# Graph attention, second sweep: edge product with edges on partitions, gathered rows added by VectorE

## What is computed

```python
h = layernorm(x) * gamma + beta
x_j, x_i = h[src], h[dst]
t = gelu(concat([x_j, edge_vector], 1) @ Wt + bt)
q = x_i @ Wq + bq
k = t @ Wk + bk
attn = sum(k * q, -1) * edge_type / sqrt(D)
m = segment_max(attn, dst)
e = exp(attn - m[dst])
a = e / (segment_sum(e, dst) + 1e-16)
aggr = segment_sum(a * (t @ Wv + bv), dst)
return residual + gelu(aggr)
```

## Time and profile before

| what | value |
|---|---|
| median of 3 runs | 4536.91 us (4527.91 to 4538.68) |
| profiled execution | 4530.53 us |
| its span, first to last instruction | 4528.9 us |
| TensorE busy, weight loads | 76%, 59% |
| GpSimd, VectorE, ScalarE busy | 68%, 42%, 35% |
| mean granted TensorE clock | 0.748 |
| DMA | 99 GB/s on average |

### The profile page before, as it was taken

How to read it: one execution, slowest core, us unless ns; L and a number is a source line. 1 busy time by engine, 2 the same in 40 slices (tenths; PEclk the granted TensorE clock), 3 DMA queues, 4 the chain that set the end, 5 groups by cost and what they waited for, 6 DMA issues and landing times. The chain is left out here.

```text
span 4528.9 us, 75426 instructions
## 1 busy us (share of the span) xinstructions
PE 3448.6 (76%) x19146; PEld 2674.6 (59%) x19147; DVE 1900.2 (42%) x6965; ACT 1604.3 (35%) x3258; POOL 3095.4 (68%) x3340
## 2 busy tenths in 40 slices
PE   1477677777767677675878888888888888888887
PEld 1356555555555555553666666666666666666665
DVE  5333222222222222223555555555555554545544
ACT  5433222222222222223434334334334334343343
POOL 7467777777777777774766666666666666666662
PEclk5566555555555655656999999999999999899998
DMA  5223323333233232333444434444434434444442
GB/s 159 66 75 85 80 76 80 78 77 80 75 80 79 77 80 75 80 79 85 124 112 115 118 115 115 117 115 116 117 113 117 118 110 120 109 116 117 114 115 67
DMA packets 390323, 446.83 MB, mean 99 GB/s; under 512 B 111896, under 2 KB 314862, under 8 KB 390256
## 3 DMA queue, kind: packets, MB, share of 16 engines
q0 software_dynamic: 100352, 205.72, 18.3%
q1 hardware_dynamic: 276940, 233.83, 17.4%
q10 hardware_dynamic: 12964, 6.53, 0.5%
HBM read 387.58 MB, written 58.21 MB: 98 GB/s over the span
## 5 line engine op out<-in xcount | busy, mean ns | idle before, releaser
L513 POOL DMA_INDIRECT attention_t<-source_rows,attention_idx x1552 | 1536.1, 990 | 493.9 <-issue 492.8
L513 POOL DMA_INDIRECT gin_hs<-h_rows,gin_idx x1472 | 1407.0, 956 | 435.8 <-issue 435.8
L678 PE MATMUL gin_sums<-gin_hot,gin_hs 128*128 128x40 f32 x3136 | 684.8, 412 | 0.0
L678 PEld LDWEIGHTS gin_sums<-gin_hot,gin_hs 128*128 128x128 f32 x3136 | 670.3, 329 | 22.4 <-issue 21.7
L1206 ACT ACTIVATE attention_tT<-attention_pre_ps 128x512 f32<-128x512 f32 x392 | 234.0, 597 | 1229.1 <-PE attention_pre_ps L1096 1229.0
L1096 PE MATMUL attention_pre_ps<-attention_evT,attention_w_edge 128*128 128x512 f32 x784 | 466.6, 681 | 2.6 <-DMA attention_evT<-in_edge_attr_cols 2.6
L1119 PE MATMUL attention_sc_q<-attention_qw,attention_tT 128*128 x3136 | 419.0, 278 | 0.0
L1119 PEld LDWEIGHTS attention_sc_q<-attention_qw,attention_tT 128*128 128x128 f32 x3136 | 400.1, 200 | 0.0
L1153 PE MATMUL attention_sum_ps<-attention_e_hot,attention_t 128*128 128x96 f32 x3136 | 389.1, 284 | 0.0
L1153 PEld LDWEIGHTS attention_sum_ps<-attention_e_hot,attention_t 128*128 128x128 f32 x3136 | 373.1, 199 | 12.3 <-issue 0.2
L1351 DVE TENSOR_TENSOR attention_masked<-attention_masked,attention_row_bank 128x80 f32<-128x80 f32 x784 | 126.3, 230 | 596.0 <-PE attention_row_bank L1141 595.7
(11 more groups left out here) (184 smaller groups left out, 5417.9 us busy)
## 6 DMA issues: line engine op xcount, KB each, us to landing
attention_evT<-in_edge_attr_cols SPq DMA_DIRECT2D x196, 512.0 KB
attention_t<-source_rows,attention_idx POOLq DMA_INDIRECT x1552, 2.6
gin_hs<-h_rows,gin_idx POOLq DMA_INDIRECT x1472
attention_qw<-qk_cols SPq DMA_DIRECT2D x98, 160.0 KB
attention_cw<-qk_bias_cols SPq DMA_DIRECT2D x98, 132.0 KB
attention_fade<-fades SPq DMA_DIRECT2D x98, 132.0 KB
gin_x<-in_x SPq DMA_DIRECT2D x98, 128.0 KB
residual_rows<-gin_r SPq DMA_DIRECT2D x98, 128.0 KB, 2.0
```

Source lines behind the costliest of these rows:

```text
L513: gp.indirect_dma_start(out=out[:, k, :], out_offset=None, in_=rows[:, :], compute_op=op, in_offset=bass.IndirectOffsetOnAxis(ap=idx[:, k: ...
L678: mm = pe.matmul(sums[j][:, bass.ds(off, WIN)], hs[bk.k][:, k, :], hot[j][:, k, :], start=False, stop=True, skip_group_check=True)
```

## The change

In words: for each quad, `edges` makes the edge product with four 128-column tiles of `evT` as stationary operands and `w_edge` moving, so that edges lie on partitions, like the gathered rows. VectorE adds the gathered rows to it (`add_rows`), from `pre_ps` and `t` into `t`. ScalarE applies GELU in `t`, in place. TensorE turns `t` once (`turn_gelu`), and ScalarE copies the result to `tT` for the scores. The 16 turnings of gathered rows per chunk fall away. TensorE's and VectorE's steps are written in another order. SyncE stores first and asks for the residual rows of chunk `c4` in place of `c5`. The other queues and GpSimd's program are the same.

```diff
 SyncE:
     def step(f, mid, late, last, c4, c5, c6):
+        if c6:
+            store(c6)
         if f:
             loads(f)
         if last:
             spread_fade(last)
-        if c6:
-            store(c6)
-        if c5:
-            own_rows(c5)
+        if c4:
+            own_rows(c4)
 TensorE:
+    def edges(f, q):
+        if q % 2 == 0:
+            wait(pe, ev_in[q // 2], 16 * (f.c + 1))
+        wait(pe, s["x_sb"], QUADS * f.c + q)
+        for k in range(4):
+            mm = pe.matmul(pre_ps[:, k * P:(k + 1) * P],
+                           evT[q // 2][:, 512 * (q % 2) + k * P:512 * (q % 2) + (k + 1) * P], w_edge[:, :],
+                           start=True, stop=True)
+        mm.then_inc(s["pre_ps"], 1)
+
+    def turn_gelu(f, q):
+        wait(pe, s["t_sb"], QUADS * f.c + q + 1)
+        wait(pe, s["tT_sb"], QUADS * f.c + q)
+        for k in range(4):
+            mm = pe.transpose(t_ps[:, k * P:(k + 1) * P], t[f.k][:, 4 * q + k, :], g["ident"][:, :])
+        mm.then_inc(s["t_ps"], 1)
...
     def step(f, mid, late, last, e):
         if f:
             load_offsets(pe, pe_regs[f.k], g, f.c)
-            turn_rows(f, 0)
+            edges(f, 0)
         if mid:
             turn_scores(mid)
         if f:
-            turn_rows(f, 1)
+            edges(f, 1)
             turn_gelu(f, 0)
-            scores(f, 0)
         if mid:
             spread_maxima(mid)
+        if f:
+            edges(f, 2)
+            turn_gelu(f, 1)
+            scores(f, 0)
         if e:
             end_products(e)
         if f:
-            turn_rows(f, 2)
-            turn_gelu(f, 1)
+            edges(f, 3)
+            turn_gelu(f, 2)
             scores(f, 1)
-            turn_rows(f, 3)
-            turn_gelu(f, 2)
+            turn_gelu(f, 3)
             scores(f, 2)
-            turn_gelu(f, 3)
-            scores(f, 3)
         if mid:
             spread_running(mid)
+        if f:
+            scores(f, 3)
         if late:
             sums(late)
 ScalarE:
     def gelu(f, q):
-        wait(act, s["pre_ps"], QUADS * f.c + q + 1)
-        act.activation(tT[q % 2][:, :], pre_ps[:, :], ACT.Gelu).then_inc(s["tT_sb"], 1)
+        x = t[f.k][:, 4 * q:4 * q + 4, :].rearrange("p k d -> p (k d)")
+        wait(act, s["x_sb"], QUADS * f.c + q + 1)
+        act.activation(x, x, ACT.Gelu).then_inc(s["t_sb"], 1)
 VectorE:
+    def add_rows(f, q):
+        x = t[f.k][:, 4 * q:4 * q + 4, :].rearrange("p k d -> p (k d)")
+        wait(v, gathered[f.k][q], 64 * (f.g + 1))
+        wait(v, s["pre_ps"], QUADS * f.c + q + 1)
+        v.tensor_tensor(x, pre_ps[:, :], x, ALU.add).then_inc(s["x_sb"], 1)
...
     def step(f, mid, late, last, e):
+        if f:
+            add_rows(f, 0)
         if last:
             add_sums(last)
         if f:
-            misses(f)
+            add_rows(f, 1)
         if mid:
             block_maxima(mid)
+        if f:
+            misses(f)
+            add_rows(f, 2)
+        if mid:
             offs = raise_maxima(mid)
+        if f:
+            add_rows(f, 3)
         if e:
             end_inverse(e)
         if mid:
             below_maxima(mid, offs)
```

More of the change, by code:

```diff
@@ L978, in attention_sweeps @@
         wgt_in = st.sem2("wgt_in")
-        names = ("pre_ps", "tT_sb", "t_ps", "t_sb", "sc_q", "miss", "biased", "prod", "score", "attn", "masked", "xm", "xm_ps",
+        names = ("pre_ps", "tT_sb", "t_ps", "t_sb", "sc_q", "x_sb", "miss", "biased", "prod", "score", "attn", "masked", "xm", "xm_ps",
                  "bm", "bm_ps", "mold", "raised", "mnew_ps", "mdiff", "kept", "fade", "below", "e_hot",
@@ L1111, in scores @@
                         c, h, j = f.c, f.h, f.j
+                        wait(pe, s["tT_sb"], QUADS * c + q + 1)
                         if q == 0:
```

19 lines of the change are left out of this document (1 added, 18 removed).

## The result

| | before | changed |
|---|---|---|
| median of the runs | 4534.43 us (4527.91 to 4538.68, 4 runs) | 4811.95 us (4811.2 to 4816.34, 4 runs) |
| ratio | | 1.0615, 95% interval 1.0597 to 1.0634 |
| profiled span | 4528.9 us | 4810.8 us |
| pairwise maxima apart, mean of 97 | 24.30 us | (4772.1 - 2143.8) / 97 = 27.10 us |
| granted clock, 2500 to 4300 us | 0.93 | 0.81 |

The median before has one run more here than the median of three above. The change costs 277 us where a gain of 183 us was forecast (4530.5 - 4347). Nearly all of it lies in the second sweep: 97 x (27.10 - 24.30) = 272 us.

What follows compares the result with a forecast made beforehand. TensorE and VectorE wait for each other in a ring of 23.39 us, 24.30 a chunk with the clock. A new ring of 21.9 plus 0.45 for the clock gives 22.35; 94 chunks save 183 us from 4530.5: 4347 us (4250 to 4440).

Steps and rivals of the forecast that it cites:

- Edge product: TensorE's product for each quad of edges: 0.94 us in place of 1.29, saving 1.4 us a chunk.
- VectorE's add: VectorE's adding of gathered rows, four a chunk: 0.70 us each, two or three of them on the ring.
- GELU from SBUF: ScalarE's in-place GELU of 512 columns: 0.64 us, costing 0.04 us a chunk, 4 us in all.
- The new ring: The chain of waits from one turning of maxima to the next: 21.8 us, TensorE's own sequence 21.9; 21.9 taken.
- Residual rows: Asked for a chunk earlier, so VectorE's subtraction runs straight into the residual sum: 1.19 us, then 0.62 to scoring.
- Queues: SyncE's new order and GpSimd's gathers: 21.0 us a chunk, 21.2 with the hold, under the ring, costed at nothing.
- Clock: TensorE's half-clock stretches: 0.45 us a chunk in place of 0.9, since each new idle place is shorter.
- Rival 5: Slower: the single PSUM buffer makes TensorE stop and go, the clock halves more often; 25.3 a chunk, 4624 us, chance 0.06.
- the sum: The total over the second sweep: 94 periods going from 24.30 to 22.35 us, a gain of 183 us.

Runs made afterwards that it cites:

- e1: The changed kernel with eight extra 128-column products, results unread, between the second scores and the last turning; 4368.97 us, ratio 0.9662.
- e18: The changed kernel with ScalarE's third copy ahead of its fourth GELU and the closing GELUs, and four unused products before the last turning; 4268.47 us.
- e4: The changed kernel with SyncE's order of before; 4808.43 us, ratio 1.0633.
- e3: The kernel before with SyncE's new order alone (store first, residual rows for one chunk further on); 4223.01 us, ratio 0.9349.
- e17: The kernel before with SyncE's new order and 20 unused small copies on ScalarE ahead of the copy of the third turned quad; 4683.08 us, ratio 1.036.
- e12: The changed kernel with four unused products before the turning of the block maxima, none before the last turning; ratio 1.063, on a run with late gathered rows.
- e14: The changed kernel with four unused products before the turning of the block maxima, run again; ratio 1.061, again with late gathered rows.
- e2: The changed kernel with ScalarE's third copy ahead of its fourth GELU and of the closing GELUs; 4405.52 us, ratio 0.9736.

## Why the prediction was wrong

It said 4347 us (4250 to 4440), with 0.06 for slower. By its own steps:

- *Edge product* (0.94 a quad): right. 3312.33 to 3313.26 is 0.93. The rule of the Trainium skill (TensorE: Matmul & The Clock Gate, Part 3, "The mechanism"), by which it would have been 1.8, did not hold here: the loads hide, as the prediction had argued from the sums' row.
- *VectorE's add* (0.70) and *GELU from SBUF* (0.64): right, 687 and 630 ns.
- *The new ring* (21.8 to 21.9): right, apart from 0.5 (0.7 in the mean, 22.59). e1 has 14.54 to the spreading (14.5) and 22.39 in all; the rest lies behind the spreading, where TensorE needs 7.85 in place of 7.4. e18, whose last turning starts 1.1 us earlier (12.01 after the turning of maxima, 13.11 in e1), makes a chunk in 21.57.
- *Residual rows*: the wait went as forecast, but not on the changed kernel's account: there it would have gone anyway (e4).
- *Queues*: GpSimd was forecast at 21.0 a chunk. e3, where it alone sets the pace, has 21.09. In the changed kernel GpSimd's wait for the sums grew in place of shrinking (6.2 us a chunk, about 1 forecast), since the sums ran at half clock.
- ***Clock*: this step failed.** It read "I expect half of them, 0.45, since each new idle place is shorter". The low stretches came to 10.2 us in a chunk of 27.1 (a clock of 0.81 over the sweep), where the kernel before has 3.4 in 24.3, and cost 27.10 - 22.59 = 4.5 us a chunk (e1 against the changed kernel), where 0.45 was forecast. Of the two idle places one, of 2.45 us, does all of it. Before the change the long idle place, 3.0 us in the median, stood ahead of the turning of maxima and the next quads. Now it stands ahead of scores, spreading and sums, and the low clock lasts until shortly before the end of the sums. Two things changed: there are three times as many microseconds at half clock, and each costs 4.5 / 10.2 = 0.44 us where by the prediction's own reading it had cost 0.9 / 3.4 = 0.26. That a shorter pause costs less was assumed, from one stretch, and no row showed it.

Rival 5 came true in its sign and its arithmetic, at 0.06. It had "from 13.1 us on all 8.8 us of TensorE's work are on the ring, so a microsecond at half clock costs half of one", and "It decides from 2 x (24.3 - 21.9) = 4.8 us at half clock a chunk". With 10.2 us that gives 21.9 + 5.1 = 27.0, and 27.1 was measured. That it comes so near is partly luck: the ring is 0.7 longer than 21.9, and the low clock costs 4.5 and not 5.1. The rival was priced with two stretches of 3.4 us. Its picture was not right, though: no stop and go at the single PSUM buffer, but one pause per chunk. The rule cited there (the Trainium skill, TensorE: Matmul & The Clock Gate, "A second HAM failure mode: psum-queue depth-cycling") speaks of short, frequent idles between groups of products. The changed kernel's trace does not bear it out as the cause there: all 66 falls begin behind the one pause of 2.45 us, and with that pause shortened to 0.63 or 0.43 us (e1, e18) none is left, though the shorter pauses stay. The old data path is another matter: the 18 falls of e3, with no pause above 0.77 us, agree with the rule.

A second thing was missed, which the sum could have told. It gave the whole gain, 1.95 us a chunk, to the change as one. Its own layout had the data path cost the ring 1.4 us, while the late residual rows alone were 2.27 us of waiting. Done alone these lines were the better kernel by 124 us than even the forecast for both.

Left open: how short an idle place before the last turning must be to be safe. In the changed data path 0.35 to 0.72 us had no fall (e1, e18), 1.30 to 1.44 sometimes, 2.3 to 2.5 in every chunk looked at; in the old one 2.63 us had one in every chunk (e17), and there were falls with no pause above 0.77 us (e3). So the pause is what decides in the changed kernel, and not the only thing that can bring the clock down. Open too is why 1.5 us ahead of the block maxima does nothing. That the low stretch lasts 3.4 us in one place and 10.2 in another was seen, in the kernel before and the changed one; what in the work behind the pause sets its length was not tested. Whether useless products would help elsewhere in the chunk as well was not settled either (e12, e14); that a shorter pause helps without them is shown by e2.

## What to carry to other kernels

Price the place of a pause, not only its length: a pause of 2.45 us in front of a long run of matmuls that others wait for cost 4.5 us here, where one of about 3 us in front of other work had cost 0.9, and filling it with useless products, or moving one copy ahead of a GELU, gave back some 400 us. Read for each new idle place which work of TensorE comes next, cost all of it once at half clock, and make that a case with a real chance. And cost the parts of a change apart: here one part was worth 302 us alone and nothing in company.

## What the runs showed that was not expected

- The clock stays at half through 10.24 us in which TensorE is busy for all 10.24. Being busy with scores and sums did not bring it back at once; it was back at 1.00 for the last 1.6 us of the sums.
- The longer pause had the shorter fall: about 3 us before the turning of maxima, then 3.4 us at half clock in 49 of 55 falls; 2.45 us before the last turning, then 10.2 us in 60 of 66.
- Useless work at the right place is a gain: 1.9 us of products per chunk (8 x 0.235) for 4.5 us of time.
- A change of four lines in the order of DMA requests moved the kernel by 6.5%, more than the 2.27 us of visible wait (97 x 2.27 = 220 us), since most of the falls of the clock went as well.
- The same kernel took 4525 and 6170 us on different occasions, with late gathered rows, in the traces of the edited kernels, as the visible difference.
